# Routing and first metric woven into the projection units, expert matrices made per batch inside the chunk loop

## The reference, cut to what matters

```
h = layernorm(x)*(1+ca) + sa
q = relu(h @ enc_q); v = relu(h @ enc_v)            # 8 heads of 16
sig = q.mean(T) + 0.5*q[::8].mean(T)                # a whole batch goes into it
metric = softplus(base + 0.1*(gelu(sig@w1+b1)@w2+b2))
per token and head: distances to the 64 tokens before it under metric,
  the 32 nearest, weights exp(-dist), a weighted sum of v; plus a Hebbian term
x = x + ga * (q*context) @ decoder
h = layernorm(x)*(1+cb) + sb
gates = softmax of the top 2 of h[:,0] @ Wr.T       # token 0 of each batch only
x = x + gb * (h + sum_e gates_e * (h @ A_e.T) @ Bw_e.T)
```

## Time and profile before

| | |
|---|---|
| three runs | 821.3, 822.74, 823.1 us, median 822.74 |
| profiled execution | 822.05 us, its span 820.0 us |
| busy share | DVE 94%, PE 86%, ACT 81%, POOL 57% |
| granted PE clock, mean | 0.96 of full |
| DMA | 27.2 MB, 33 GB/s |

### The profile page before, as it was taken

One profiled execution on the slowest core, in us unless ns is written; L12 is line 12 of the kernel. 1 busy time (PEld: TensorE's weight loads), 2 busy tenths in 40 slices (PEclk: granted clock), 3 DMA queues, 4 the chain that ended last, 5 costly groups with the idle time before them and its releaser, 6 DMA issues.

```text
span 820.0 us, 21167 instructions
## 1 busy us (share of the span) xinstructions
PE 705.0 (86%) x4437; PEld 578.9 (71%) x4437; DVE 768.8 (94%) x6618; ACT 666.4 (81%) x2054; POOL 465.4 (57%) x871
## 2 busy tenths in 40 slices
PE   5987989888889888888898888889888888888845
PEld 3445677777777777777777777777777777777744
DVE  5966999999999999999999999999999999999980
ACT  3981368988888889888888988888888888888964
POOL 2112456666666666666666666666666666666531
PEclk9995999999999999999999999999999999999955
DMA  5310001001111100111110011111100111110000
GB/s 169 106 29 12 24 24 30 24 29 32 32 31 31 30 25 27 32 32 32 31 32 29 22 30 32 32 32 30 30 27 27 32 31 32 31 31 27 23 4 10
DMA packets 49231, 27.23 MB, mean 33 GB/s; under 512 B 5512, under 2 KB 48592, under 8 KB 49104
## 3 DMA queue, kind: packets, MB, share of 16 engines
q1 hardware_dynamic: 49104, 25.90, 10.7%
HBM read 10.28 MB, written 4.19 MB: 18 GB/s over the span
## 4 chain that ended last, share of the span: by engine, by line
DVE 87%; PE 6%; DMA 2%; ACT 2%; issue 1%; SPq 0%; POOL 0%; ACTq 0%
DVE work L982 47%; DVE m L971 31%; DVE key L1004 5%; DMA big<-in_x 2%; DVE key L793 1%; PE psD L1052 1%; DVE big L949 1%; DVE st_p L784 1%; DVE den L1014 1%; PE psC L1177 1%; PE psD L1147 1%; PE psC L1080 1%; DMA wmod_sb<-in_wmod 1%; DVE rden L1021 0%; PE psW L1046 0%
## 5 line engine op out<-in xcount | busy, mean ns | idle before, releaser
L982 DVE MATCH_REPLACE8 work<-m,work 128x64 f32<-128x64 f32 x1536 | 302.5, 211 | 0.0
L1147 PE MATMUL psD<-sst,tst 128*128 128x224 f32 x1024 | 238.8, 356 | 0.0
L971 DVE MAX8 m<-work 128x8 f32<-128x64 f32 x1536 | 212.0, 212 | 0.0
L1147 PEld LDWEIGHTS psD<-sst,tst 128*128 128x128 f32 x1024 | 196.1, 192 | 3.1 <-issue 0.3
L452 POOL TENSOR_TENSOR big<-work,con 128x512 f32<-128x512 f32 x128 | 162.1, 1288 | 12.3 <-ACT work L635 11.6
L481 POOL TENSOR_TENSOR t<-cst,qh 128x128 f32<-128x128 f32 x64 | 27.7, 432 | 226.0 <-ACT cst L715 226.0
L1177 PE MATMUL psC<-vst,big 128*128 128x34 f32 x1024 | 127.1, 270 | 0.0
L1177 PEld LDWEIGHTS psC<-vst,big 128*128 128x128 f32 x1024 | 126.5, 195 | 0.2
L982 DVE MATCH_VALUE_LOAD work<-m,work 128x8 f32 x1536 | 123.1, 80 | 0.0
L982 DVE MATCH_REPLACE8 work<-m,key 128x64 f32<-128x64 f32 x512 | 100.4, 211 | 0.0
L1144 PE MATMUL psD<-mask_bf,ident_bf 128*128 128x448 bf16 x256 | 91.0, 355 | 1.8 <-DMA tst<-nst 1.8
(11 more groups left out here) (200 smaller groups left out, 1464.8 us busy)
## 6 DMA issues: line engine op xcount, KB each, us to landing
hst<-hT_all SPq DMA_DIRECT2D x64, 96.0 KB
tst<-qT_all SPq DMA_DIRECT2D x256, 17.0 KB
big<-in_x SPq DMA_DIRECT2D x16, 256.0 KB, 2.8
tst<-nst SPq DMA_DIRECT2D x256, 1.0 KB
xs<-in_x SPq DMA_DIRECT2D x64, 64.0 KB, 1.9
out<-yo SPq DMA_DIRECT2D x64, 64.0 KB, 1.7
sst<-nst SPq DMA_DIRECT2D x128, 3.0 KB
con<-in_consts SPq DMA_DIRECT2D x1, 549.5 KB, 5.5
```

The lines of the kernel that those rows point to most:

```text
L971: last = v.max(m8[:, h], src[:, h * WIN:(h + 1) * WIN])
L982: last = v.match_replace(work[:, s, cols], m8[:, h], src[:, cols], GONE)
L1147: last = mm(bank_of(r)[:, g, 0:SW], tst[:, s, r, g], sst[:, s, g], start=False, stop=(g == NG - 1), skip_group_check=True)
```

## The change

**Units.** The ring `xp` has eight buffers, `xn` four (`key` and `work`). Normalising goes from DVE to POOL, as x*rs + nb with nb made on DVE (`nbias`). The Ln and Exp of the inverse deviation are now one call, `invstd`. `con` is loaded in two parts, c comes first.

**Routing.** Token 0 of the eight batches is normalised and projected by itself ahead of the units, so that its attention and the routing need not wait for them. Their instructions stand in `unit_extra(n)` behind unit n, on PE, ACT and DVE. The metric is made in two parts: batch 0 in units 2 to 6, batches 1 to 7 in the chunk loop (gelu at step 1, exponentials at 2, the rest on POOL in steps 3 and 4).

**First chunks.** Norms and values of chunks 0 and 1 are made in units 10 to 13. The loop starts at step -1 in place of -3, and chunk 0's distances are computed ahead of it.

**Expert matrices.** The scaling of all batches' rows and the 16 wide matmuls are gone. In every batch POOL scales one batch's rows in `expert_rows` (before step 8b-1) and `gated_expert_rows` (before step 8b), PE multiplies in `experts` (step 8b+2), ACT copies the result (step 8b+3).

```diff
+RING = 8
+        xp = big[:].rearrange("p a s (u c d) -> p (a s u) c d", u=2, c=4)
@@ SP
+            def load(n):
+                need(sync, xn_ready, n - RING + 1)
+                sync.dma_start(xp[:, n % RING], xh[:, n]).then_inc(xp_in[n % RING], 16)
...
@@ POOL
+            def normalise(n):
+                u = n % RING
+                pool.wait_ge(nb_ready, n + 1)
+                need(pool, pT_ready, n - 3)
+                for c in range(4):
+                    last = nc.gpsimd.tensor_scalar(xn(n)[:, c], xp[:, u, c], rs_p[:, u, c:c + 1],
+                                                   nb_p[:, u, c:c + 1], ALU.mult, ALU.add)
+                last.then_inc(xn_ready, 1)
...
+            def expert_rows(b):
+                need(pool, pG_ready, b)
+                nc.gpsimd.tensor_tensor(bs[:], b_sb[:], gate_er[:, :, b:b + 1].broadcast_to([P, 4, D]), ALU.mult).then_inc(bs_ready, 1)
+            def gated_expert_rows(b):
+                pool.wait_ge(bs_ready, 3 * b + 1)
+                nc.gpsimd.tensor_tensor(bs[:], bs[:], g_b[:, b:b + 1].broadcast_to([P, 4, D]), ALU.mult).then_inc(bs_ready, 1)
+                nc.gpsimd.tensor_tensor(gI[:], ident, g_b[:, b], ALU.mult).then_inc(bs_ready, 1)
...
+            for i in range(FIRST, LAST + 1):
+                if i == FIRST:
+                    pool.wait_ge(r0_dve, 10)
+                    pool.wait_ge(ab_in, 32)
+                    pool.wait_ge(gatew_ready, NB // 2)
+                if (i + 1) % CPB == 0 and i + 1 < NCH:
+                    expert_rows((i + 1) // CPB)
+                if i % CPB == 0 and 0 <= i < NCH:
+                    gated_expert_rows(i // CPB)
+                if i == 3:                      # four small instructions on sp
...
+                if i == 4:                      # six, the last one writes aS of batches 1 to 7
...
@@ ACT
+                if n == 3:
...
+                    gelu(0, psC)
...
+                if n == 6:
+                    act.wait_ge(r0_dve, 4)
...
+            for n in range(NU):
+                if n + 1 < NU:
+                    to_hT(n + 1)
+                to_q(n)
+                if n + 4 < NU:
+                    invstd(n + 4)
+                unit_extra(n)
...
+                if i % CPB == 3 and i < NCH:
+                    b = i // CPB
+                    act.wait_ge(pG_ready, b + 1)
+                    nc.scalar.activation(g_b[:, b], pY, ACT.Copy).then_inc(gb_ready, 1)
...
+                if i == 1:
+                    gelu(1, psX)
+                if i == 2:
+                    exp_of_abs(1, psX)
...
@@ DVE
+            for n in range(NU):
+                if n + 3 < NU:
+                    nbias(n + 3)
+                unit_extra(n)
+                if n + 6 < NU:
+                    stats(n + 6)
...
+                if i == 0:
+                    gate_weights(3)
...
@@ PE
+            def to_pT(n):
                 pe.wait_ge(xn_ready, n + 1)
                 need(pe, hT_ready, n - 1)
+                if n in (12, 14):
+                    pe.wait_ge(n2_ready, n // 2 - 5)
+                if n in (13, 15):
+                    pe.wait_ge(vst_ready, n // 2 - 5)
...
+            def experts(b):
+                pe.wait_ge(bs_ready, 3 * b + 3)
+                for kt in range(4):
+                    mm(pY, a_sb[:, kt], bs[:, kt], start=(kt == 0), stop=False)
+                mm(pY, ident, gI[:], start=False, stop=True).then_inc(pG_ready, 1)
...
+            for n in range(NU):
+                if n + 1 < NU:
+                    to_pT(n + 1)
+                to_pq(n)
+                unit_extra(n)
...
+            distances(0, 0)
+            distances(0, 1)
+            pe.wait_ge(q_ready, 4 * NB)
+            distances(0, 2)
+            distances(0, 3).then_inc(dist_ready, 1)
+            gate_rows(3)
```

More of the change, by code:

```diff
@@ L314, in need, with there, metric @@
                 eng.wait_ge(s, value)
[L316 to L329, removed]
+        ROWS_IN = 16 * (NR + NG + NR)
+        FIRST, LAST = -1, NCH + 2
+        NU = 2 * NB
+        METRIC = (slice(0, 1), slice(1, NB))
+        def there(i, off, first=0):
+            return first <= i + off < NCH
         def column(k):
             return k * CH + (k // CPB) * WIN
+        def metric(j, part):
+            return sp[:, j].rearrange("p (g b) -> p g b", g=NG)[:, :, METRIC[part]]
         block = ctx.enter_context(nc.Block())
@@ L370, in step @@
                     sync.dma_start(oc[:, k], yo[:, s]).then_inc(out_in[s], 16)
[L372 to L394, removed]
+                if there(i, 3, 2):
+                    windows(i + 3)
+                    norms(i + 3)
+            for i in range(FIRST, LAST + 1):
+                step(i)
             for s in range(2):
@@ L1023, in step @@
                 replaces(i, 3, 1)
-            steps(step, routing)
+            for i in range(FIRST, LAST + 1):
+                if i == 0:
+                    gate_weights(3)
+                if i == 4:
+                    dve.wait_ge(sp_pool, 2)
+                    v.reciprocal(metric(5, 1), metric(5, 1)).then_inc(sp_dve, 1)
+                step(i)
         @block.tensor
@@ new lines, in metric_2, with values @@
+            def metric_2(part, bank):
+                pe.wait_ge(h1_ready, part + 1)
+                for g in range(NG):
+                    last = mm(bank[:, 64 + g * NB:64 + (g + 1) * NB][:, METRIC[part]], w2_sb[:, g], h1[:, METRIC[part]],
+                              start=True, stop=True)
+                last.then_inc(pm2_ready, 1)
+            def values(k):
+                s = k % 2
+                pe.wait_ge(hst_in[s], 16 * (k // 2) + 16)
+                need(pe, vst_ready, k)
+                need(pe, wts_ready, 2 * (k - 2))
+                for v in range(2):
+                    last = mm(pV[:, v], hst[:, s, v * WIN:(v + 2) * WIN], encv_sb[:], start=True, stop=True)
+                last.then_inc(v_ready, 1)
@@ new lines, in norms @@
+            def norms(k):
+                s = k % 2
+                pe.wait_ge(opnd_ready, 2 * (k + 1))
+                need(pe, n2_ready, k)
+                need(pe, wts_ready, 2 * k - 7)
+                for g in range(NG):
+                    mm(pN, selm[:, s, g], sqs[:, s, g], start=(g == 0), stop=(g == NG - 1))
+                for g in range(NG):
+                    last = mm(pNN, sqs[:, s, g, WIN:3 * WIN], seln[:, g], start=(g == 0), stop=(g == NG - 1))
+                last.then_inc(pn_ready, 1)
@@ L1214, in step @@
                     distances(s, 0)
-                k, s = i + 2, (i + 2) % 2
-                if there(i, 2):
-                    need(pe, vst_ready, k)
-                    need(pe, wts_ready, 2 * (k - 2))
-                    for v in range(2):
-                        last = mm(pV[:, v], hst[:, s, v * WIN:(v + 2) * WIN], encv_sb[:], start=True, stop=True)
-                    last.then_inc(v_ready, 1)
+                if there(i, 2, 2):
+                    values(i + 2)
                 k, s = i + 2, (i + 2) % 2
```

793 lines of the change are left out of this document (445 added, 348 removed).

## The result

| | before | after |
|---|---|---|
| median of four runs | 822.92 us (821.3 to 824.8) | 844.13 us (842.9 to 845.1) |
| profiled execution, its span | 822.05, 820.0 | 845.04, 843.3 |
| granted PE clock, mean | 0.96 | 0.94 |

The ratio is 1.0259, 95% interval 1.0242 to 1.0275. The kernel is 2.6% slower; the forecast was 821.4 us.

A forecast was written before the change was run, and what follows sets the result against it. DVE was taken to bound the loop, busy 11.00 of 11.00 us a chunk. 820.0 - 7.65 - 3.3 + 4.65 + 5.6 = 819.3 us of span, so 821.35 us; range of 8 in 10, 814 to 828.

The forecast's parts named there:

- The start: DVE's first MAX8 of the loop at 82.0 us, 7.65 earlier; bounds 77 and 88, right between 80 and 84.
- end of unit 9: Units 0 to 9 ahead of the loop, at 2.44 us a unit on ACT plus woven-in work, end at 53.7 us.
- The first steps of the loop: Steps 0 to 4: added delays less their cover cost 4.65 us together, bounds 1 and 9; 3.3 of expert matrices go.
- The second wait that the prediction excluded: In the chunk loop DVE waits only at L1004, for qh of ACT; waits at other places would prove it wrong.
- the 18 that I had put down as a refutation: DVE's waits at L1004 in the loop: a sum under 3 or over 18 us would prove the prediction wrong.
- Each batch: Batches 1 to 7: expert work on POOL and PE costs DVE 0.8 us a batch, 5.6 in all; bounds 0 and 15.
- In step 0: PE's norms of chunk 2 wait for POOL's squares behind the expert rows; chunk 1's distances at 86.8, costing 1.35 us.
- The rule weighed: ACT's table switches: a drain of about 1.38 us follows each 1.28 us load, giving 826.9 us; given no chance.
- Normalising on GpSimd: Units: four POOL instructions at 0.43 us, 1.7 a unit, hidden under ACT's 2.44; wrong if over 0.6 each.
- The rivals: Loop hides additions, 815.6 us (0.22); units pack better, 817.8 (0.14); slower batch turns, 827.0 (0.18); late loop start, 825.9 (0.12).
- The slower one: Turn of each batch: POOL's three instructions and PE's ten passes cost DVE 1.6 us a batch, 827.0 us; chance 0.18.
- All five cases: The forecast of no change that can be told (chance 0.34) and its four rivals, from 815.6 to 827.0 us.

The follow-up runs named there:

- e1: Kernel after, with filler matmuls added at the head of PE's steps where it idles (steps -1 to 4, 8b, 8b+1), no work removed or moved: 834.8 us.
- a2: Kernel after, with the expert rows of batches 1 to 7 scaled on GpSimd behind the squares of the same step, not ahead of it: 831.6 us.
- a1: Kernel after, with GpSimd scaling batch 0's expert rows at the head of step 1, not at steps -1 and 0: 844.0 us.
- d1: Kernel after with metric's second part two steps earlier and expert rows behind the squares, plus five ACT delays (2 to 10 copies, steps 18 to 50): 844.6 us.
- d3: d1 with the same five delays, plus 6 to 28 filler matmuls on PE at the head of each delayed step, ahead of its first wait: 830.5 us.

## Why the prediction was wrong

**The start was right.** 83.28 for 82.0, inside 80 to 84. By its steps: first projection 15.59 (forecast 15.2), end of unit 9 about 54.2 (53.7), unit 13's transposes 61.01 (60.4), chunk 0's distances ready 79.45 (78.1), from there to MAX8 3.8 (3.75). A few rows of PE's timeline:

```profile
15.59 2.75 PE L1202 MATMUL psD<-hT_all,encq_sb 128*128 128x512 f32 x4
...
61.01 0.63 PE L1195 MATMUL psW<-con,key 128*128 128x128 f32 x4 [0.46 <-ACT vst L692]
...
78.53 0.92 PE L1345 MATMUL psD<-sst,tst 128*128 128x224 f32 x4
```

The 0.7 us between 61.0 and 79.4 and the 0.6 before it are all that it missed.

**The first steps of the loop failed.** The prediction had 1.35 in step 0, 1.4 in step 1, 0.3, 1.4 and the reciprocal, "together 4.65 us, bounds 1 and 9"; it measured 20.5 (2.1 in chunk 0 and 18.4 in chunks 1 to 6), over twice the upper bound. Each term was a delay less its cover, and it took every engine's durations as they are at full clock. With PE's clock held, e1 shows 4.0 for chunks 1 to 6 and 1.2 for chunk 0, 5.2 in all, so the sum of delays was sized well and the missing term is what they do to PE's clock: 20.5 - 5.2 = 15.3 us. The prediction put it at nothing without naming it. PE's waits in steps 0 and 1 (timeline):

```profile
92.14 0.36 PE L1342 MATMUL psD<-mask_bf,ident_bf 128*128 128x448 bf16 x1 [2.90 <-DMA tst<-nst]
...
103.18 1.11 PE L1361 MATMUL psW<-con,big 128*128 128x128 f32 x4 [3.66 <-POOL big L569]
```

The gelu with its table loads holds up ACT's Square and Exp of the weights (the first began at 100.91, behind the second load), these the unfold, and PE idles 3.66 us. Four transposes then took 1.11 us, where they take 0.66 at full clock. The trace before had held the pattern. Its windows of chunks 2 and 3, which the prediction did not look at:

```profile
108.90:119.91 11.01, 9.85 (x55) 8.14 (x54) 11.01 (x101) 6.59 (x19) 7.04 (x13) 0.85 0.06 18
119.91:131.15 11.24, 10.60 (x76) 9.22 (x76) 11.24 (x100) 10.43 (x33) 7.04 (x13) 1.00 0.11 30
```

The clock was 0.85, 3.3 us at half, and the two chunks together cost 0.25 us over 22.0: PE's slack covered that stretch. I had read the clock of one steady chunk, 1.00, and took it for the loop.

The second wait that the prediction excluded also came: DVE's `den` waits for `cst` of ACT, 6.4 us in five of the chunks (the other 9.6 are at the end, where before had 9.2). That the contexts come late from a slow PE is my reading; no run tests it. And L1153's waits add up to 24.7, of which 3.5 lie ahead of the first MAX8; the 21.2 left are past the 18 that I had put down as a refutation.

**Each batch was right, except for two.** Forecast 0.65 + 0.05 + 0.1 = 0.8 a batch; measured 0.50 (chunk 8b), 0.11 (8b+1) and 0.18 (8b+4), 0.79 in all, 5.5 for seven. Two of the turns cost 3.0 and 3.3 us more, 6.3 in all, by half clock. The prediction had no term for that either. Both parts went when GpSimd's three instructions moved (a2), with the reserve said there.

**In step 0** I had PE's norms wait for GpSimd's squares behind the expert rows; a1 moved the rows and nothing changed. What made chunk 1's distances late is in PE's rows:

```profile
82.17 1.68 PE L1345 MATMUL psD<-sst,tst 128*128 128x224 f32 x4
...
87.05 0.92 PE L1345 MATMUL psD<-sst,tst 128*128 128x224 f32 x4
```

The first two of four parts ran at half clock, and the last ended at 88.91, not at 86.8. So the 1.35 was near e1's 1.2 by luck: the cause it was worked out from isn't there.

**The rule weighed.** The gelu's table load in unit 3 began at 35.45, and ACT's next activation at 36.75, 1.30 later: the trace agrees with 1.28 us a load and not with a drain behind it.

**Normalising on GpSimd** took 0.46 to 0.47 us an instruction (0.43 taken); behind unit 0 PE waited for it once, 0.41 us.

**The rivals.** None was it. The slower one, 1.6 us a batch, named the turns, where 11.8 us were lost, and had the wrong mechanism for the part above 0.8: it too let a late engine cost only its lateness. None named the first steps of the loop. All five cases shared the assumption that failed, so the range, 814 to 828, held only cases at full clock.

The Trainium skill describes the mechanism (TensorE: Matmul & The Clock Gate, HAM oscillation — how this bites in real kernels): a wait for data between bursts throttles PE, the next burst starts slow, and the penalty is the throttled time times one half. By the rows above chunks 0 to 6 hold 2 x (1 - clock) x length = 37 us at half clock, 18.5 us of lost PE work by that formula; 15.3 were paid. In d1 one chunk pair had 2 x (0.14 x 15.18 + 0.29 x 16.17) = 13.6 us, 6.8 by the formula, and lost 5.6 against d3. The trace agrees in kind, and the formula is above the price both times; that PE's slack took the difference is my reading. Had I used it, the fill would have had a term for the clock.

## What to carry to other kernels

Where PE is busy most of a step (here 9.8 of 11.0 us), read its granted clock by stretch before pricing any delay: a delay that lets PE stand idle can be paid twice, once for its length and once for the slow stretch behind it. Put added work of other engines where they idle behind what PE waits for, not at the head of a step, and try whether cheap matmuls in PE's idle time, ahead of the wait and not behind it, hold the clock. A cost that is the same in each batch by the code need not be the same by the clock.

## What the runs showed of the hardware

- In the doses, idle times of PE of 2.52 us and more were followed by half clock each time, the one of 1.42 was not. At the turns, with waits of 1.18 or 1.19 and 0.46 us close together, it fell at batch 1 and not at batch 2, and at batch 3 behind 1.48 and 0.47; in e1, with 0.99 and 0.47, it held at chunk 9 and fell at chunk 41. With the same code there it fell at none to three of seven turns, by the run.
- A stretch at half clock of some 3.4 us (d1's second, third and fifth delay) cost 0.9 to 1.1 us, one of 13.6 us 5.6.
- The mask matmul of 128x448 in bf16 took 0.21 us each in a row of seven, though the row of a single one reads 0.35 or 0.36: the duration of one matmul is more than what it adds to a row of them.
